# Second-layer logits as wide matmuls in one PSUM bank, W2's preparation later, and more attention weights made ahead

## The chip, the cores and the metric

One core of a Trainium2 chip. The metric is device time in microseconds (us) of one execution of the whole program; three runs of the kernel before gave 1488.98, 1492.28 and 1493.37, median 1492.28.

## The reference, cut to what matters

A graph attention network of two layers and then a mixture-of-experts feed-forward block, both added to their input. N = 1250 nodes, 20,000 edges and a self loop for each node, D = 768 features.

```python
def _gat_layer(x, src, dst, W, a_src, a_dst, bias, concat):
    N = x.shape[0]
    H, C = a_src.shape                    # layer 1: 4 heads of 512; layer 2: 1 head of 768
    h = (x @ W).reshape(N, H, C)
    al_s = jnp.einsum('nhc,hc->nh', h, a_src)
    al_d = jnp.einsum('nhc,hc->nh', h, a_dst)
    e = jax.nn.leaky_relu(al_s[src] + al_d[dst], NEG_SLOPE)
    m = jax.ops.segment_max(e, dst, num_segments=N)
    ex = jnp.exp(e - m[dst])
    denom = jax.ops.segment_sum(ex, dst, num_segments=N)
    alpha = ex / (denom[dst] + 1e-16)
    out = jax.ops.segment_sum(h[src] * alpha[:, :, None], dst, num_segments=N)
    ...
h   = jax.nn.elu(_gat_layer(x, src, dst, W1, att_src1, att_dst1, b1, concat=True))
out = _gat_layer(h, src, dst, W2, att_src2, att_dst2, b2, concat=False)
```

The change concerns the hand-over between the layers: the second layer's logits `al_s` and `al_d`, and the preparation of W2. As `h @ W2` is only needed for its product with the two attention vectors, the kernel computes `v = W2 @ a` once and gets the logits as `h1 @ v`, from the first layer's output `h1`, without the projection.

## The kernel before, in words

All edges are held in a dense count matrix CT (node by node), so attention is a dense matmul: P is the exponential of the leaky sum, times CT, and a head's output is P times its projected features. Every large f32 operand is split into a high and a low f16 half, and a product is three matmuls (`mm3`: high by high, high by low, low by high).

Nodes are ten tiles of T = 125. The destinations of a head are three blocks of 500, 375 and 375 columns (`DB`, and `TB` in tiles: four, three and three). A head's period has NG = 15 groups on TensorE: for each block one group of denominators (20 matmuls against ones) and four of attention (CH = 4 chunks of 128 features, each 30 matmuls). Groups 0, 5 and 10 are the denominators. Before the groups of head h, TensorE projects head h + 1 (`proj`); the last head has none ahead of it. Each group writes one of four banks in turn, so TensorE may be four groups ahead of VectorE, which reads them (`den_read`, `att_read`).

The order of work on each engine is written out by hand; an engine does its list in order, and waits on semaphores.

- `p_steps(h, n)` makes n more steps of P for head h: one step is a tile of 125 sources by one block, 30 tiles in 32 steps of a pipeline that goes ScalarE (L913, sum), VectorE (L1306, leaky maximum), ScalarE (L919, exponential), VectorE (L1314, times the counts), ScalarE (L931, high half), VectorE (L1321, low half). `CUR_STEPS[h][g]` says how many steps of the present head are made in group g, `NEXT_STEPS[g]` how many of the next.
- For an attention group VectorE divides (L1357), ScalarE makes a relu and an exponential (L956, L958), VectorE the ELU (L1364), ScalarE and VectorE the high and low half of h1 (L969, L1372) into `H1O`, of which there are two, one for each block in turn. SP stores them to memory (L569), and ScalarE waits for the store of two blocks ago and for `al2` of it before it writes again.
- `chain_row`, `chain_max` (L1285, ten a head) and `chain_shift` (L1291 to L1295) make the next head's row of logits and the shift of the softmax, over TensorE's transposes (L1690, L1694) and SP's broadcasts through memory. TensorE's transpose for the shift stands in front of group 8. P of the next head can begin when the shift rows are back.
- `al2(k)` is the second layer's logits of block k (12 in all): for each tile of the block and each of the four chunks, three matmuls of the 128 by 125 part of h1 against the two columns of `V2S`, into bank 4. VectorE adds them to `A2C` (`a2_add`, L1380). It stands in front of the third group (c == 1) of the next block.
- `load_w2(ch)` (SP, L597), `w2_hi(ch)` (ScalarE, L977) and `w2_lo(ch)` (VectorE, L1385) bring one of W2's 16 chunks of 128 rows into one of three slots `W2G` and split it. `w2_at` places them: seven in groups 8 to 14 of the last but one head, nine in groups 0 to 8 of the last. A slot is loaded again once the chunk three before it is split.
- Behind attention TensorE projects h1 by W2, tile by tile (96 matmuls of 384 columns for each of ten), the first tile chunk by chunk as the split ones come. `al2` of the last block stands in the middle of the first tile (chunk 8), the transpose for the second layer's row (`chain_row(H)`) at its chunk 12, that for the shift behind the third tile. Then VectorE's `chain_max(H, j)` needs the masks, which SP loads into the place of the W2G slots, so behind the last `w2_lo`. SP's list also loads h1 back, tile by tile (L658).

After that come the second attention, the router and the nine feed-forward networks, which the change does not touch.

## Time and profile before

| | |
|---|---|
| median of three runs | 1492.28 us |
| profiled execution, its own time | 1488.8 us |
| its span | 1487.0 us |
| mean granted TensorE clock | 0.94 |
| TensorE matmuls busy | 1290.4 us, 87% |
| VectorE busy | 931.1 us, 63% |
| ScalarE busy | 595.8 us, 40% |
| narrow logit matmuls, 480 | 37.6 us busy |

"Busy" is the union of an engine's instructions. A row of the timeline merges instructions of one line that follow each other; its first number is where it starts in the span, its second how long it lasts, and the brackets say how long the engine stood idle before it and who released it. The granted clock is a share of 2.4 GHz: 0.5 is the lower of its two levels, 1.2 GHz, and a value between is a mean over time.

### The profile page before, as it was taken

Reading aid. Unit: us, or ns where it says so; the run is one execution under the profiler, and the core shown is the slowest. Engines: PE = TensorE matmul, PEld = TensorE weight load, DVE = VectorE, ACT = ScalarE, POOL = GpSimd, SP = SyncE. Lnnn points to the kernel's source line nnn. Section 1 sums busy time; section 2 is a strip of 40 time slices with the busy share of each in tenths; the row PEclk is TensorE's granted clock in tenths of the full one; section 3 lists DMA queues with packets and bytes.
Section 4 is the critical chain, followed back from the end, with each engine's and each line's share of the span. In section 5 each row is a group of like instructions: output and inputs, shape, how many; then the busy total and the mean of one; then the engine's idle time right before and its main releaser. Section 6 shows DMA issues by size and latency. Waiting matters only on the chain.

```text
span 1487.0 us, 19887 instructions
## 1 busy us (share of the span) xinstructions
PE 1290.4 (87%) x7482; PEld 843.1 (57%) x7482; DVE 931.1 (63%) x1863; ACT 595.8 (40%) x1025; POOL 256.5 (17%) x187
## 2 busy tenths in 40 slices
PE   1574897678899898986889999999999989999996
PEld 1342344335555565553357888888854756666664
DVE  6578996599788968867872446335468623333330
ACT  1344215566565455537752046300141124444441
POOL 1398200000000000000000000040001453344322
PEclk9987899798899899998889999999989989999999
DMA  8442201413520353134123431061220267667622
GB/s 206 166 147 78 69 0 46 135 45 110 153 92 29 103 152 94 36 87 125 54 98 103 151 117 56 16 194 35 81 86 1 61 204 190 175 181 179 165 57 29
DMA packets 71441, 152.71 MB, mean 103 GB/s; under 512 B 10837, under 2 KB 34901, under 8 KB 70730
## 3 DMA queue, kind: packets, MB, share of 16 engines
q1 hardware_dynamic: 64699, 134.28, 30.2%
q0 software_dynamic: 6656, 17.26, 6.0%
q8 instruction: 57, 0.93, 0.3%
q14 instruction: 29, 0.24, 0.1%
HBM read 118.93 MB, written 34.59 MB: 103 GB/s over the span
## 4 chain that ended last, share of the span: by engine, by line
PE 55%; DVE 17%; ACT 8%; issue 7%; DMA 6%; POOL 5%; SPq 1%; DVEq 0%; POOLq 0%; ACTq 0%
PE PS L1650 41%; PE PS L1767 5%; PE PS L1713 5%; DVE sb L1285 3%; POOL sb L762 3%; DVE sb L1306 2%; DVE sb L1314 2%; DVE sb L1194 1%; DMA sb<-in_x_dram 1%; ACT sb L931 1%; DVE sb L1321 1%; DMA h_d<-sb 1%; ACT sb L919 1%; ACT sb L913 1%; DVE sb L1357 1%
## 5 line engine op out<-in xcount | busy, mean ns | idle before, releaser
L1650 PE MATMUL PS<-sb,sb 128*125 128x384 f16 (+9 forms) x4884 | 822.4, 326 | 84.7 <-DVE sb L1199 25.9
L1650 PEld LDWEIGHTS PS<-sb,sb 128*125 128x125 f16 (+3 forms) x4884 | 579.1, 132 | 318.5 <-issue 71.7
L1767 PE MATMUL PS<-sb,sb 125*128 125x375 f16 (+1 forms) x1440 | 277.7, 356 | 0.0
L1767 PEld LDWEIGHTS PS<-sb,sb 125*128 125x128 f16 x1440 | 146.2, 102 | 124.8 <-issue 20.9
L774 POOL TENSOR_TENSOR sb<-sb,sb 125x768 f32<-125x768 f32 x10 | 18.0, 1840 | 807.7 <-DMA sb<-in_x_dram 807.7
L919 ACT ACTIVATE sb<-sb 125x375 f32<-125x375 f32 (+1 forms) x150 | 81.6, 544 | 112.8 <-DVE sb L1306 112.3
L1494 DVE SCALAR_TENSOR_TENSOR sb<-sb,sb 128x2304 f16<-128x2304 f32 x27 | 68.8, 2557 | 89.2 <-ACT sb L1052 89.2
L1713 PE MATMUL PS<-sb,sb 125*125 125x500 f16 x320 | 88.6, 417 | 12.6 <-DVE sb L1237 12.6
L1306 DVE SCALAR_TENSOR_TENSOR sb<-sb,sb,sb 125x375 f32<-125x375 f32 (+1 forms) x150 | 95.8, 640 | 3.3 <-ACT sb L913 2.9
L1237 DVE TENSOR_SCALAR sb<-sb,sb 125x500 f16<-125x500 f16 x320 | 95.5, 383 | 3.3 <-PE PS L1713 3.3
L913 ACT ACTIVATE sb<-sb,sb 125x375 f32<-125x375 f32 (+1 forms) x150 | 93.7, 628 | 8.0 <-DMA sb<-aa_d 8.0
L1194 DVE CUSTOM_DVE_ANT_0 sb<-PS,sb 125x512 f16<-125x512 f32 x80 | 55.2, 690 | 55.7 <-ACT sb L871 54.3
L1314 DVE SCALAR_TENSOR_TENSOR sb<-sb,sb 125x375 f32<-125x375 f32 (+1 forms) x150 | 87.7, 584 | 1.2 <-ACT sb L919 1.1
L1321 DVE TENSOR_TENSOR sb<-sb,sb 125x375 f16<-125x375 f32 (+1 forms) x150 | 87.9, 586 | 0.3
L762 POOL TENSOR_TENSOR sb<-sb,sb 128x768 f32<-128x768 f32 x32 | 78.0, 2470 | 55.7 <-DMA sb<-in_L_gnn_W_dram 47.6
L931 ACT ACTIVATE sb<-sb 125x375 f16<-125x375 f32 (+1 forms) x150 | 81.8, 545 | 12.0 <-DVE sb L1314 11.7
L1285 DVE CUSTOM_DVE_ANT_0 sb<-sb,sb 125x1250 bf16<-125x1250 bf16 x50 | 71.1, 1456 | 17.3 <-ACT sb L988 10.1
L1713 PEld LDWEIGHTS PS<-sb,sb 125*125 x320 | 40.1, 141 | 60.9 <-issue 40.9
L794 POOL TENSOR_TENSOR sb<-sb,sb 128x392 f16<-128x392 f32 (+2 forms) x33 | 30.8, 932 | 203.4 <-ACT sb L1070 203.4
L1624 DVE TENSOR_TENSOR sb<-PS,sb 128x588 f16<-128x588 f32 x32 | 23.8, 767 | 66.3 <-ACT sb L1092 66.3
L956 ACT ACTIVATE sb<-sb,sb 128x375 f32<-128x375 f32 (+1 forms) x48 | 30.8, 642 | 80.8 <-DVE sb L1357 80.7
L1070 ACT ACTIVATE sb<-sb 128x392 f16<-128x392 f32 (+2 forms) x33 | 17.7, 536 | 108.6 <-DVE sb L1515 108.6
(185 smaller groups left out, 1092.9 us busy)
## 6 DMA issues: line engine op xcount, KB each, us to landing
sb<-in_L_ffn_w_dram SPq DMA_DIRECT2D x24, 1152.0 KB, 5.7
sb<-xt_d SPq DMA_DIRECT2D x40, 375.0 KB, 3.9
sb<-in_L_gnn_W_dram SPq DMA_DIRECT2D x32, 384.0 KB, 3.2
sb<-mask_d SPq DMA_DIRECT2D x20, 546.9 KB
sb<-h_d SPq DMA_DIRECT2D x10, 1000.0 KB, 5.4
h_d<-sb SPq DMA_DIRECT2D x16, 375.0 KB, 5.0
sb<-aa_d SPq DMA_DIRECT2D x5, 1093.8 KB
sb<-in_L_gnn_W_dram SPq DMA_DIRECT2D x18, 256.0 KB, 3.8
```

The costliest lines, as they stand in the source:

```text
L762: nc.gpsimd.tensor_tensor(VP[a][:, :], WV[ch % 3][:, :], A2R[:, a, :], ALU.mult).then_inc(s_vp, 1)
L913: A(TMP[:, q % NTMP, 0:n], ROW[:, 1, lo:lo + n], ACT.Identity, bias=ALF[:, h, i:i + 1]).then_inc(s_p1, 1)
L919: A(TMP[:, q % NTMP, 0:n], TMP[:, q % NTMP, 0:n], ACT.Exp).then_inc(s_p3, 1)
L931: A(P[:, i, 0, lo:lo + n], TMP[:, q % NTMP, 0:n], ACT.Copy).then_inc(s_p5, 1)
L1237: V.tensor_scalar(OR[:, n % RO, :], iok[:, :], 1000.0 * c, KEY[:, bass.ds(col, 1)], ALU.add, ALU.is_equal).then_inc(s_or, 1)
L1285: V.tensor_tensor_reduce(junk, mask, max_row(h), 1.0, 3.0 * NEG, ALU.add, ALU.max, MX[:, j:j + 1]).then_inc(s_mu, 1)
L1306: V.scalar_tensor_tensor(TMP[:, q % NTMP, 0:n], ROW[:, 0, lo:lo + n], AL[:, 0, h, i:i + 1], TMP[:, q % NTMP, 0:n], ALU.add, ALU.max).then_ ...
L1314: V.scalar_tensor_tensor(TMP[:, q % NTMP, 0:n], TMP[:, q % NTMP, 0:n], 1.0, CT[:, i, lo:lo + n], ALU.min, ALU.mult).then_inc(s_p4, 1)
L1321: V.tensor_tensor(P[:, i, 1, lo:lo + n], TMP[:, q % NTMP, 0:n], P[:, i, 0, lo:lo + n], ALU.subtract).then_inc(s_p6, 1)
L1650: ins = M(out_, lhs(a), rhs(b), start=first and a + b == 0, stop=last and a == 1)
L1713: ins = M(PS[0:T, c, 0:KC], OL[:, bass.ds(col, 1), :], OR[:, n % RO, :], start=q == 0, stop=q == len(jobs[c]) - 1)
L1767: ins = M(PS[:, t, 0:n], hb[:, i, pa, 128 * c:128 * c + 128], P[:, i, pb, lo:lo + n], start=i == 0 and pa + pb == 0, stop=i == NT - 1 and ...
```

## The change

1. `al2(k)` turns its operands round: `V2S`, set into a row of 20 columns of which only 8 to 11 are not zero, is the stationary operand with 12 columns, cut so that block b's four sums (high and low part of two vectors) land on partitions 4b to 4b + 3; the moving operand is h1, with all tiles of the block (500 or 375 columns) at once. A block is 8 matmuls, and all 12 blocks are added up in bank 4, with no read between. `a2_add` and `A2C` are gone. It now stands in front of the block's fifth group (c == 3).
2. At the end, VectorE copies the 12 by 500 sums (`A2W`), ten f32 matmuls with a selection matrix `SEL` (made by GpSimd at the start) turn them into columns, and VectorE scales these. These matmuls stand in the second tile of the second projection (chunk 2), `chain_row(H)` at its chunk 6; `al2` of the last block at chunk 4 of the first tile.
3. W2's chunks 0 to 7 are split in groups 7 to 14 of the last head, 8 to 15 behind the last group. SP's loads, stores and the loads of h1 are put in another order to match.
4. The last head's P: 13 steps made in the period before instead of 9, then 2 instead of 4 before its groups, then 3, 3, 3, 3, 2, 2, 2 instead of 4, 4, 3, 3, 3, 3.

```diff
-    V2S = small([128, NCH, 2, 2], F16)
+    V2S = small([128, NCH, 20], F16)
+    SEL = small([12, NB, 2], F32)
...
-                     [4, 4, 3, 3, 3, 3, 0, 0, 0, 0, 0, 0, 0, 0, 0]]
+                     [3, 3, 3, 3, 2, 2, 2, 0, 0, 0, 0, 0, 0, 0, 0]]
...
-        NEXT_STEPS = [0, 0, 0, 0, 0, 0, 0, 0, 0, 0, 1, 2, 2, 2, 2]
+        NEXT_STEPS = [[0, 0, 0, 0, 0, 0, 0, 0, 0, 0, 1, 2, 2, 2, 2],
+                      [0, 0, 0, 0, 0, 0, 0, 0, 0, 0, 1, 2, 2, 2, 2],
+                      [0, 0, 0, 0, 0, 0, 0, 0, 0, 0, 2, 2, 3, 3, 3]]
+        W2_EARLY = 8
...
-            if h == H - 2:
-                return range(g - 8, g - 7) if g >= 8 else range(0)
-            if h == H - 1:
-                return range(min(7 + g, NCH), min(8 + g, NCH))
+            if h == H - 1 and g >= NG - W2_EARLY:
+                return range(g - NG + W2_EARLY, g - NG + W2_EARLY + 1)
+            if h == H:
+                return range(W2_EARLY, NCH)
...
             load_ht(0)
+            for ch in range(6, 8):
+                load_w2(ch)
             store_h1(NB * H - 2)
+            for ch in range(8, 11):
+                load_w2(ch)
             load_ht(1)
+            load_w2(11)
+            store_h1(NB * H - 1)
+            for ch in range(12, NCH):
+                load_w2(ch)
+            load_ht(2)
             sp.wait_ge(s_w2l, NCH)
             for t in range(2):
                 load_masks(H, t)
-            store_h1(NB * H - 1)
             chain_row(H)
-            load_ht(2)
             load_ht(3)
...
-                    p_steps(h, 4)
+                    p_steps(h, 2)
...
-                    if c == 1 and NB * h + b:
-                        a2_add(NB * h + b - 1)
...
+            for ch in w2_at(H, 0):
+                w2_lo(ch)
+            dve.wait_ge(s_a2, NB * H)
+            V.tensor_copy(A2W[:, :], PS[0:12, 4, 0:500]).then_inc(s_a2r, 1)
+            dve.wait_ge(s_a2c, 1)
+            AC = PS[0:T, 5, 0:2 * NT].rearrange("p (j a) -> p a j", a=2)
+            V.tensor_scalar(AL[:, :, H, :], AC, 1.0 / (SX * SW), None, ALU.mult).then_inc(s_a2r, 1)
             chain_row(H)
...
                 pe.wait_ge(s_y6, CH * (k + 1))
-                if k:
-                    pe.wait_ge(s_a2r, k)
-                for j in range(len(TB[b])):
-                    for c in range(CH):
-                        ins = mm3(PS[0:T, 4, 2 * j:2 * j + 2], lambda a: H1O[k % 2][:, a, j, c, :],
-                                  lambda r: V2S[:, CH * h + c, r, :], c == 0, c == CH - 1)
+                for c in range(CH):
+                    for part in range(2):
+                        ins = M(PS[0:12, 4, 0:n], V2S[:, CH * h + c, 8 - 4 * b:20 - 4 * b],
+                                H1O[k % 2][:, part, 0:nj, c, :], start=k + c + part == 0,
+                                stop=k == NB * H - 1 and c == CH - 1 and part == 1)
                 ins.then_inc(s_a2, 1)
+
+            def al2_columns():
+                pe.wait_ge(s_a2r, 1)
+                for b in range(NB):
+                    for j in TB[b]:
+                        lo = T * (j - TB[b].start)
+                        ins = M(PS[0:T, 5, 2 * j:2 * j + 2], A2W[:, lo:lo + T], SEL[:, b, :], start=True, stop=True)
+                ins.then_inc(s_a2c, 1)
...
-                    if c == 1 and NB * h + b:
+                    if c == CH - 1 and NB * h + b:
                         al2(NB * h + b - 1)
...
-                        if ch == NCH // 2:
+                        if ch == 4:
                             al2(NB * H - 1)
-                        if ch == NCH - 4:
+                    if j == 1:
+                        if ch == 2:
+                            al2_columns()
+                        if ch == 6:
                             chain_row(H)
```

Elsewhere, SP's list for the last two heads loses the loads of chunks 3 to 15 (chunks 3 to 5 stand behind the store of the last head's first block), and a constant of the expert stage (`io392`) moves to a place that is free by then.

## Rows read from the trace of the kernel before

**Rows 1.** The page's chain that ended last, shares of the span by engine.

```profile
PE 55%; DVE 17%; ACT 8%; issue 7%; DMA 6%; POOL 5%; SPq 1%; DVEq 0%; POOLq 0%; ACTq 0%
```

**Rows 2.** Busy time by stretch, us: PE, PEld, DVE, ACT, POOL, PEclk, DMA share, GB/s.

```profile
654.00:694.00 40.00, 36.79 (x233) 22.45 (x232) 21.50 (x36) 19.98 (x35) 0.00 (x0) 0.91 0.52 147
694.00:715.00 21.00, 8.00 (x25) 1.86 (x23) 19.03 (x33) 16.75 (x32) 0.00 (x0) 0.65 0.32 93
```

**Rows 3.** Timeline of TensorE, heads 1 and 2: start, us, what, count, idle before.

```profile
470.88 2.19 PE L1650 MATMUL PS<-sb,sb 128*125 128x2 f16 x36
...
502.74 5.28 PE L1650 MATMUL PS<-sb,sb 128*125 128x2 f16 x48 [2.70 <-DVE sb L1372]
507.88 7.14 PE L1767 MATMUL PS<-sb,sb 125*128 125x375 f16 x30
...
518.11 11.40 PE L1767 MATMUL PS<-sb,sb 125*128 125x375 f16 x60
...
564.46 4.07 PE L1650 MATMUL PS<-sb,sb 128*125 128x512 f16 x18 [2.72 <-DVE sb L1199]
...
653.62 9.72 PE L1767 MATMUL PS<-sb,sb 125*128 125x375 f16 x60
...
674.55 2.61 PE L1650 MATMUL PS<-sb,sb 128*125 128x2 f16 x36 [3.21 <-DVE sb L1372]
```

**Rows 4.** The same view for the last head and the first projection tile.

```profile
704.24 1.01 PE L1762 MATMUL PS<-sb,sb 125*128 125x500 f16 x2 [4.09 <-DVE sb L1321]
...
714.83 7.66 PE L1767 MATMUL PS<-sb,sb 125*128 125x500 f16 x30
...
724.39 19.14 PE L1767 MATMUL PS<-sb,sb 125*128 125x500 f16 x90
...
758.33 5.28 PE L1650 MATMUL PS<-sb,sb 128*125 128x2 f16 x48 [6.83 <-DVE sb L1372]
763.47 16.91 PE L1767 MATMUL PS<-sb,sb 125*128 125x375 f16 x90
...
790.27 14.56 PE L1767 MATMUL PS<-sb,sb 125*128 125x375 f16 x90
804.66 13.95 PE L1650 MATMUL PS<-sb,sb 128*125 128x384 f16 x108
```

**Rows 5.** Timeline of VectorE: the divisions that begin a group, heads 1 and 3.

```profile
479.46 0.68 DVE L1357 TENSOR_TENSOR sb<-PS,sb 128x500 f32<-128x500 f32 x1 [2.84 <-PE PS L1767]
...
551.16 0.55 DVE L1357 TENSOR_TENSOR sb<-PS,sb 128x375 f32<-128x375 f32 x1
...
556.19 0.55 DVE L1357 TENSOR_TENSOR sb<-PS,sb 128x375 f32<-128x375 f32 x1
...
743.68 0.67 DVE L1357 TENSOR_TENSOR sb<-PS,sb 128x500 f32<-128x500 f32 x1
...
751.78 0.67 DVE L1357 TENSOR_TENSOR sb<-PS,sb 128x500 f32<-128x500 f32 x1
```

**Rows 6.** Timeline of ScalarE: the first W2 chunk, in head 2.

```profile
669.35 0.84 ACT L977 ACTIVATE sb<-sb 128x768 f16<-128x768 f32 x1 [7.93 <-DMA sb<-in_L_gnn_W_dram]
```

**Rows 7.** Groups by line: busy us, mean ns; idle before and its releasers.

```profile
L762 POOL TENSOR_TENSOR sb<-sb,sb 128x768 f32<-128x768 f32 x32 | 78.0, 2470 | 55.7 <-DMA sb<-in_L_gnn_W_dram 47.6 <-ACT sb L875 8.1
...
L1385 DVE SCALAR_TENSOR_TENSOR sb<-sb,sb 128x768 f16<-128x768 f32 x16 | 15.3, 959 | 18.0 <-ACT sb L977 18.0
...
L977 ACT ACTIVATE sb<-sb 128x768 f16<-128x768 f32 x16 | 13.2, 827 | 7.9 <-DMA sb<-in_L_gnn_W_dram 7.9
...
L1718 PE MATMUL PS<-sb,sb 125*128 125x1 f32 x2 | 0.4, 260 | 1.1 <-DVE sb L1245 1.1
```

**Rows 8.** The 16 loads of W2 chunks (line 597), from issue to landing.

```profile
DMA to landing us min/median/max: 2.8/3.4/8.2
```

**Rows 9.** Timeline of VectorE: a mask wait, and what follows the layer-two shift.

```profile
834.89 1.46 DVE L1285 CUSTOM_DVE_ANT_0 sb<-sb,sb 125x1250 bf16<-125x1250 bf16 x1 [4.37 <-DMA sb<-mask_d]
...
846.60 0.95 DVE L1443 SCALAR_TENSOR_TENSOR sb<-PS,sb 125x768 f16<-125x768 f32 x1
```

More of the change, by code:

```diff
@@ L132, in build @@
     assert o <= 207008, o
+    A2W = at(o_a - 2016, [12, 500], F32)
     WV = [at(o_e + 3072 * b, [128, D], F32) for b in range(3)]
@@ L185, in build @@
     ones = small([T, 128], F16)
-    io392 = small([T, SLOTS], F16)
+    io392 = at(o_w2s + 30720, [T, SLOTS], F16)
     io8 = small([T, E], F32)
@@ L197, in build @@
     V2F = small([128, NCH, 2], F32)
-    V2S = small([128, NCH, 2, 2], F16)
+    V2S = small([128, NCH, 20], F16)
+    SEL = small([12, NB, 2], F32)
     AL = small([T, 2, H + 1, NT], F32)
     ALF = small([T, H + 1, NT], F32)
-    A2C = small([T, 2 * NT], F32)
     MX = small([T, NT], F32)
@@ L346, in build @@
         s_a2 = sem("al2_part_done")
-        s_a2r = sem("al2_part_added")
+        s_a2r = sem("al2_rows_kept_then_scaled")
+        s_a2c = sem("al2_columns_done")
+        s_vs = sem("v2_split")
         s_w2g = [sem(f"w2_in_slot{b}") for b in range(3)]
@@ L628, in _ @@
                             load_xt(h + 2, i)
-                    else:
-                        for ch in range(3, 7):
-                            load_w2(ch)
                     store_h1(NB * h + 1)
                 else:
-                    for ch in range(7, 10):
-                        load_w2(ch)
                     store_h1(NB * h - 1)
-                    for ch in range(10, 14):
-                        load_w2(ch)
                     store_h1(NB * h)
-                    for ch in range(14, NCH):
+                    for ch in range(3, 6):
                         load_w2(ch)
@@ L752, in _ @@
                                 allow_small_or_imprecise_dtypes=True))
+            link(nc.gpsimd.memset(SEL[:, :, :], 0.0))
+            for part in range(2):
+                link(nc.gpsimd.affine_select(out=SEL[:, :, :], in_=SEL[:, :, :], compare_op=ALU.not_equal, fill=1.0,
+                                             base=-2 * part, pattern=[[-4, NB], [-1, 2]], channel_multiplier=1))
             pool.wait_ge(s_a2v, 32)
@@ L1021, in h2_hi @@
                   scale=1.0 / SW).then_inc(s_h2h, 1)
+            for ch in w2_at(H, 0):
+                w2_hi(ch)
             act.wait_ge(s_wrl, 16)
@@ L1268, in _ @@
             dve.wait_ge(s_va, 2 * NCH)
-            link(V.tensor_copy(V2S[:, :, 0, :], V2F[:, :, :]))
-            link(V.tensor_tensor(V2S[:, :, 1, :], V2F[:, :, :], V2S[:, :, 0, :], ALU.subtract))
-            link(V.memset(A2C[:, :], 0.0))
+            link(V.memset(V2S[:, :, :], 0.0))
+            link(V.tensor_copy(V2S[:, :, 8:10], V2F[:, :, :]))
+            V.tensor_tensor(V2S[:, :, 10:12], V2F[:, :, :], V2S[:, :, 8:10], ALU.subtract).then_inc(s_vs, 1)
             def chain_max(h, j):
@@ L1373, in h1_lo @@
                                        SX, H1O[k % 2][:, 0, 0:nj, c, :], ALU.mult, ALU.subtract).then_inc(s_y6, 1)
-            def a2_add(k):
-                j0, nj = TB[k % NB].start, len(TB[k % NB])
-                dve.wait_ge(s_a2, k + 1)
-                if k:
-                    dve.wait_ge(s_a2r, k)
-                V.tensor_tensor(A2C[:, 2 * j0:2 * j0 + 2 * nj], A2C[:, 2 * j0:2 * j0 + 2 * nj], PS[0:T, 4, 0:2 * nj], ALU.add
-                                ).then_inc(s_a2r, 1)
             def w2_lo(ch):
@@ L1393, in _ @@
                 else:
-                    p_steps(h, 4)
+                    p_steps(h, 2)
                 maxed = 0
@@ L1428, in _ @@
                         w2_lo(ch)
-            a2_add(NB * H - 1)
-            dve.wait_ge(s_a2r, NB * H)
-            link(V.tensor_scalar(AL[:, 0, H, :], A2C[:, 0:2 * NT:2], 1.0 / (SX * SW), None, ALU.mult))
-            V.tensor_scalar(AL[:, 1, H, :], A2C[:, 1:2 * NT:2], 1.0 / (SX * SW), None, ALU.mult).then_inc(s_a2r, 1)
-            dve.wait_ge(s_a2r, NB * H + 1)
+            for ch in w2_at(H, 0):
+                w2_lo(ch)
[4 more added lines that the diff above has]
+            V.tensor_scalar(AL[:, :, H, :], AC, 1.0 / (SX * SW), None, ALU.mult).then_inc(s_a2r, 1)
             chain_row(H)
@@ L1775, in al2 @@
                 h, b = divmod(k, NB)
+                n, nj = DB[b][1], len(TB[b])
                 pe.wait_ge(s_y6, CH * (k + 1))
-                if k:
-                    pe.wait_ge(s_a2r, k)
-                for j in range(len(TB[b])):
-                    for c in range(CH):
-                        ins = mm3(PS[0:T, 4, 2 * j:2 * j + 2], lambda a: H1O[k % 2][:, a, j, c, :],
-                                  lambda r: V2S[:, CH * h + c, r, :], c == 0, c == CH - 1)
-                ins.then_inc(s_a2, 1)
+                if k == 0:
+                    pe.wait_ge(s_vs, 1)
+                for c in range(CH):
+                    for part in range(2):
+                        ins = M(PS[0:12, 4, 0:n], V2S[:, CH * h + c, 8 - 4 * b:20 - 4 * b],
+                                H1O[k % 2][:, part, 0:nj, c, :], start=k + c + part == 0,
+                                stop=k == NB * H - 1 and c == CH - 1 and part == 1)
+                ins.then_inc(s_a2, 1)
+            def al2_columns():
[5 more added lines that the diff above has]
+                ins.then_inc(s_a2c, 1)
             for h in range(H):
```

12 lines of the change are left out of this document (6 added, 6 removed).

## The prediction

> **What bounds the kernel now.** I read the page's chain first: TensorE holds 55% of it, VectorE 17%, ScalarE 8% and unexplained "issue" 7% [rows 1]. So TensorE sets the end, and the only gains are stretches where it stands idle or is slow. The table by stretches shows the largest near the change [rows 2]: in the first 21 us of the last head TensorE is busy 8.0 us while VectorE is busy 19.0 and ScalarE 16.8, where the 40 us before it were nearly full. TensorE's timeline then gives each wait [rows 3, 4], VectorE's what held it [rows 5]. The reader should see three kinds. (a) Heads 0 to 2: the narrow logit matmuls wait for VectorE's last H1 piece (2.70 and 3.21 us), and group 8 waits for the softmax shift. (b) The last head's denominators wait for P (rows such as 704.24, idle 4.09), because P's makers were late: at 669.35 ScalarE had stood 7.93 us for the first W2 chunk from memory [rows 6], and each later group carries a W2 pair of 0.83 and 0.96 us [rows 7]. (c) A 6.83 us idle before the logit matmuls at 758.33. From 758 to the end of attention, 804.7, nothing but clock is lost. I write head 3 for the last head, group 0 to 14 for a head's attention groups; groups 0, 5 and 10 are denominators.
>
> **Price of the logit matmuls.** Narrow ones: 36 take 2.05 us (470.88 to the next start at 472.94, 57 ns each), 48 take 2.7; 6.8 us a head. The wide ones are in no row. Nearest are attention's own with the same 500 or 375 columns: 90 in 19.14 us, 0.21 each, and 90 in 14.56, 0.16 each [rows 4]. I take those: 8 make 1.7 us, 8 short ones 1.3, so 4.3 a head. Below, they could not well beat the narrow ones' 57 ns each (0.5 us a block); above, the f32 row of 260 ns each at one column [rows 7] would be 2.1 us a block. On the path that is under 1 us a block either way. VectorE's twelve little adds (0.15 us each by its timeline, 1.8 in all) go for nothing, since most lie beside waits. The three new GpSimd instructions and the wider split vectors stand early, ahead of work that waits 47.6 us for memory [rows 7]: nothing.
>
> **Heads 1 and 2 up to the shift.** VectorE is the bound there: after 479.46 it runs nearly without a break to the shift that releases TensorE at 518.1. But at 479.46 it stood 2.84 us for TensorE's group 2, in front of which lay the narrow block of 2.05 us [rows 3, 5]. The block moves to group 4, where VectorE is behind TensorE, so VectorE gains min(2.05, 2.84) = 2.05 us in each of heads 1 and 2, 4.1 in all. The wait of 2.70 before the block at 502.74 goes too, but gains nothing: what is late next is the shift. TensorE will stand idle there about 12 us where it had 2.7 and 3.0.
>
> **Behind the shift** the tail is TensorE's. Before it held one narrow block (2.05), now two wide ones (1.7 + 1.3): +0.95 a head. The clock is the larger matter. After 2.70 us idle the rows at 502.74 and 507.88 are 2.6 and 2.3 us longer than at full speed; after 6.83 us idle the rows at 758.33 and 763.47 are 2.6 and 2.35 longer. I take 4.5 us of such loss behind each new idle (bounds 0.1, the row 653.62 against 9.6, and 7, above any row). Behind the shift it was 1.8 in head 1 (518.11: 11.40 against 9.6) and 0.1 in head 2. Head 1: +0.95 + 2.7 = +3.65, against a projection wait of 2.72 (564.46) and a little more behind it [rows 3], which were VectorE's and come earlier with the shift: about nothing left. Head 0 has no block in group 2 and no such gain; I charge it 0.5 (bounds 0 and 5). So at the shift of head 2 the kernel is 4.1 - 0.5 = 3.6 us early: 649.9.
>
> **Head 2's tail.** The first W2 pairs leave it. TensorE: six groups of 4.8, denominators 3.2, two blocks 3.0, clock 4.4: it is through at 649.9 + 39.4 = 689.3, before the 694 of then. VectorE makes P: reads group 8 at 659.7, group 9 at 666.2, denominators at 669.6, group 11 at about 675. A group with two P steps of 500 columns and no weight work takes 5.03 us (551.16 to 556.19 [rows 5]); 1.4 of it is the group's own three operations, so a third step adds 1.8: 6.9. Group 12 at 680, 13 at 687, 14 at 693.8. The tenth tile of P, which the denominators need, is done in group 14, at 698.7; they end about 699.7, where before they ended at 715.0. TensorE still waits some 6 us here, with 13 steps made ahead instead of 9.
>
> **Head 3.** From 699.7 TensorE has 7.66 (first group, as at 714.83, clock included), 19.1, 22.4 and 22.4 for the rest, and blocks 1.3 + 1.7 + 1.3: 75.9, end at 775.6. Is anything later than that? VectorE starts group 0 at 704 with 3.2 + 3 steps; groups with three steps of 375 columns and a W2 pair last 8.1 us (743.68 to 751.78), the pair is about 1.6 of it (0.83 and then 0.96, a little overlapped), so 6.5 without. It reaches group 5 at 736, where TensorE is at 731 and may be four groups ahead; with 15 steps done at 704 and three or two a group, the P tiles for group 5 are done by 720, those for group 10 by 747 (needed at 751). W2 pairs ride in groups 7 to 14, of which each leaves 4.8 us for 4.5 of VectorE's and ScalarE's turn. So TensorE holds. The idle of 6.83 and its 4.95 us of slow clock are gone. Attention ends 804.8 - 775.6 = 29.2 us earlier.
>
> **Behind attention.** The last block is wide: -0.75. Ten small f32 matmuls for the columns: 0.26 us each at most [rows 7], half when packed: +2.0 (bounds 1 and 3). Then the W2 chunks 8 to 15. They pass through three slots, each reload waits for the pair three chunks back; SP also puts a 1 MB load of H1 and a store of 0.75 MB between chunks 10 and 12. Landing takes 2.8, 3.4 or 8.2 us (least, median, most [rows 8]). TensorE uses a chunk each 0.98 us (804.66: 108 instructions less the narrow 2.05 is 11.8 for 12 chunks) and would end the first tile 17.0 after attention. Pair 7 is done at +4.8, pairs 8 and 9 at +5.8 and +6.7, 10 at +10.3. With 3.4 for every load, chunk 15 comes at +18.2, a stall of 2.2; with 8.2 for every one, at +29, a stall of 13. I take 5.5 (the loads beside the 1 MB land late, the others near the median), and 2 for clock behind short waits. In the Trainium skill, "DMA: Bandwidth & Descriptors", section "Anatomy of one DMA", a transfer costs a fixed 2.0 us and bytes over 436 GB/s, an estimate of 2.9 us for a chunk of 0.39 MB. The least landing of the trace, 2.8, agrees; by it alone this stall would be 1.3 instead of 5.5.
>
> Last, the shift of layer two. Its row now leaves from chunk 6 of the second tile instead of chunk 12 of the first: 10 chunks less, 9.8 us, to the end of the third tile, where TensorE wants the shift. Before, VectorE was done at 846.6 [rows 9] and TensorE came at 853.8, 36 chunks of 0.98 behind 818.6 [rows 4]: 7.1 us to spare. That is 2.7 short, but the mask waits in it, 4.37 us and a shorter one, lay behind two H1 loads of 1 MB, of which one is now earlier; I take 0.5 (bounds 0 and 5). Sum behind attention: -0.75 + 2.0 + 5.5 + 2 + 0.5 = +9.25.
>
> **Sum.** 29.2 - 9.25 = 20.0 us less. The profiled execution (1488.8, span 1487.0) becomes 1468.8. It lay 3.5 us, 0.2%, under the median of the runs, 1492.28, so the median becomes 1472.
>
> **Rivals.**
> - The ring of three W2 slots: landings near 8.2 us through the stall, 13 + 5 for clock, and the shift 3 late. For it: chunk 0 took that long [rows 6, 8]. Against: most took 3.4. 29.2 - 22 = 7: 1485.
> - Better: landings near 2.8, full clock, shift in time: behind attention +3: 1466, or 1463 if the clock comes back sooner behind the shifts.
> - Slower: P still binds the last head. Its 33 steps are as many as before; four more are squeezed into head 2's tail, and if groups with three steps need 8 to 9 us there, the tenth tile comes no earlier than it did, and VectorE's lag carries through groups 5 and 10. Then 3.6 is gained in front and 9.25 lost behind: +5.6, 1498. It decides from the point at which head 3 gives back less than 9.25 - 3.6 = 5.7 us. Against: the 8.1 us groups had a W2 pair, and VectorE's three operations a step add to 1.8.
> - Slower also: the clock. The idle before each shift grows from 2 to 4 us to 9 to 12. If the clock stayed at 1.2 GHz for the whole 35 us tail of the three heads, 17.5 each instead of 4.5, less some 5 of slack: 1506. The rows show no low stretch over 10.5 us behind an idle. In the Trainium skill, "TensorE: Matmul & The Clock Gate", section "Part 1: The HAM clock gate", the half clock is the default state, which activity releases; read so, the length of the idle does not matter, the loss is as in the rows, and the sum stands.
>
> **Chances.** Forecast 0.58 (its own range 1466 to 1479); slot ring 0.17; better 0.12; P still binding 0.08; clock 0.05. The range takes in the ring and the better case: 1463 to 1485. A measurement of this kernel tells about 0.3%, 4.5 us, from nothing. Faster: the first three but for 0.02 of the ring's far end, plus mild forms of the last two, 0.86; same 0.05; slower 0.09.
>
> **What would show it.** Right: group 2's read on VectorE with under 1 us idle in heads 1 and 2; an idle of 9 to 12 us before each shift; no W2 line in head 2; the last head's denominators ending near 700; attention ending near 776; waits for the W2 pair (VectorE) in the first projection tile of 3 to 8 us; TensorE's wait at the layer-two shift under 3. Wrong: idle before group 5 or 10 of the last head; over 10 us lost in the first projection tile; a clock under 0.8 over a whole tail.

## The result, and the profile after

Four runs of the changed kernel gave a median of 1469.28 us (1465.73 to 1471.1), four of the kernel before on the same chip 1491.58: ratio 0.9848, 95% interval 0.9824 to 0.9872. The forecast was 1472. The profiled execution took 1465.73 us, its span is 1463.9, 23.1 less than before. The page's chain by engine has TensorE at 60% where it had 55 [rows 1]; its matmuls are busy 1267.5 us, 87% of the span.

The stretches of [rows 2], after:

```profile
654.00:694.00 40.00, 36.78 (x219) 20.50 (x216) 30.75 (x53) 27.87 (x53) 0.00 (x0) 1.00 0.41 107
694.00:715.00 21.00, 20.90 (x92) 9.27 (x92) 20.80 (x38) 16.66 (x36) 0.00 (x0) 0.92 0.11 37
```

In the second, TensorE is busy 20.90 of 21 us instead of 8.00. VectorE and ScalarE do about as much there as before: they are no longer late, since their busy time in the first stretch rose from 21.5 and 20.0 us to 30.8 and 27.9.

TensorE's timeline of head 1 (lines: L1771 attention, L1766 denominators, L1786 the wide block, L1698 the shift's transpose, L1654 projections), for [rows 3]:

```profile
483.79 1.45 PE L1786 MATMUL PS<-sb,sb 128*12 128x375 f16 x8
...
516.05 0.38 PE L1698 MATMUL PS<-sb,sb 125*20 125x125 f32 x1 [11.63 <-DVE sb L1308]
516.22 6.95 PE L1771 MATMUL PS<-sb,sb 125*128 125x375 f16 x30
523.10 1.86 PE L1786 MATMUL PS<-sb,sb 128*12 128x500 f16 x8
```

Head 2's tail and the last head, for [rows 4]:

```profile
649.08 0.38 PE L1698 MATMUL PS<-sb,sb 125*20 125x125 f32 x1 [8.80 <-DVE sb L1308]
649.25 6.99 PE L1771 MATMUL PS<-sb,sb 125*128 125x375 f16 x30
...
686.65 3.54 PE L1766 MATMUL PS<-sb,sb 125*128 125x500 f16 x16
692.07 0.59 PE L1766 MATMUL PS<-sb,sb 125*128 125x500 f16 x2 [1.89 <-DVE sb L1335]
694.10 0.79 PE L1766 MATMUL PS<-sb,sb 125*128 125x500 f16 x2 [1.43 <-DVE sb L1335]
694.68 20.68 PE L1771 MATMUL PS<-sb,sb 125*128 125x500 f16 x90
...
740.62 1.87 PE L1786 MATMUL PS<-sb,sb 128*12 128x500 f16 x8
742.42 4.95 PE L1771 MATMUL PS<-sb,sb 125*128 125x375 f16 x30
```

From 694.68 no row of the last head has a wait (the first 90 matmuls lose 1.5 us of clock). The waits have moved to two other places: one long idle before each shift, and the first projection tile, which before had none in 13.95 us [rows 4]:

```profile
771.10 4.07 PE L1654 MATMUL PS<-sb,sb 128*125 128x384 f16 x24
775.09 1.45 PE L1786 MATMUL PS<-sb,sb 128*12 128x375 f16 x8
776.47 7.04 PE L1654 MATMUL PS<-sb,sb 128*125 128x384 f16 x42
785.75 1.45 PE L1654 MATMUL PS<-sb,sb 128*125 128x384 f16 x6 [2.23 <-DVE sb L1391]
789.05 8.17 PE L1654 MATMUL PS<-sb,sb 128*125 128x384 f16 x36 [1.85 <-DVE sb L1391]
797.15 2.34 PE L1796 MATMUL PS<-sb,sb 12*125 12x2 f32 x20
799.41 5.80 PE L1654 MATMUL PS<-sb,sb 128*125 128x384 f16 x24
805.05 0.27 PE L1694 MATMUL PS<-sb,sb 125*10 125x125 f32 x1
805.16 25.51 PE L1654 MATMUL PS<-sb,sb 128*125 128x384 f16 x156
830.51 0.27 PE L1698 MATMUL PS<-sb,sb 125*20 125x125 f32 x1
```

Who held it is in ScalarE's timeline: the first half of a W2 pair waits for its chunk from memory, and VectorE's half (L1391) and TensorE wait behind.

```profile
778.75 0.84 ACT L989 ACTIVATE sb<-sb 128x768 f16<-128x768 f32 x1 [2.43 <-DMA sb<-in_L_gnn_W_dram]
783.86 0.84 ACT L989 ACTIVATE sb<-sb 128x768 f16<-128x768 f32 x1 [4.27 <-DMA sb<-in_L_gnn_W_dram]
787.16 0.84 ACT L989 ACTIVATE sb<-sb 128x768 f16<-128x768 f32 x1 [2.46 <-DMA sb<-in_L_gnn_W_dram]
```

The layer-two shift stands at 830.51, before at 853.66: 23.15 us, the whole gain of the span.

### The profile page after: what moved, and what is told of

The parts are those of the page before. It is cut to its first block, busy times and chain, and to the rows that moved or that the text cites. A ratio compares the mean times of both kernels' runs of the same rounds, so it can differ in the third digit from the quotient of the medians.

```text
span 1463.9 us, 19131 instructions
## 1 busy us (share of the span) xinstructions
PE 1267.5 (87%) x7118; PEld 814.8 (56%) x7118; DVE 931.5 (64%) x1851; ACT 595.6 (41%) x1025; POOL 257.6 (18%) x190
## 4 chain that ended last, share of the span: by engine, by line
PE 60%; DVE 17%; DMA 6%; ACT 6%; issue 5%; POOL 5%; SPq 1%; DVEq 0%; POOLq 0%; ACTq 0%
PE PS L1654 40%; PE PS L1771 10%; PE PS L1717 5%; DVE sb L1299 3%; POOL sb L774 3%; DVE sb L1320 2%; DVE sb L1328 2%; PE PS L1766 2%; DVE sb L1208 1%; DVE sb L1335 1%; DMA sb<-in_x_dram 1%; DVE sb L1251 1%; POOL sb L806 1%; DMA sb<-in_L_ffn_w_dram 1%; DVE sb L1371 1%
## 5 line engine op out<-in xcount | busy, mean ns | idle before, releaser
L1654 PE MATMUL PS<-sb,sb 128*125 128x384 f16 (+8 forms) x4404 | 790.1, 340 | 68.0 <-DVE sb L1213 23.4
L1654 PEld LDWEIGHTS PS<-sb,sb 128*125 128x125 f16 (+3 forms) x4404 | 543.7, 129 | 302.0 <-issue 70.7
L1771 PE MATMUL PS<-sb,sb 125*128 125x375 f16 (+1 forms) x1440 | 267.4, 347 | 0.0
L1771 PEld LDWEIGHTS PS<-sb,sb 125*128 125x128 f16 x1440 | 141.9, 99 | 121.9 <-issue 14.0
L1717 PE MATMUL PS<-sb,sb 125*125 125x500 f16 x320 | 88.6, 417 | 12.6 <-DVE sb L1251 12.6
L1084 ACT ACTIVATE sb<-sb 128x392 f16<-128x392 f32 (+2 forms) x33 | 17.7, 536 | 108.6 <-DVE sb L1519 108.6
L968 ACT ACTIVATE sb<-sb,sb 128x375 f32<-128x375 f32 (+1 forms) x48 | 30.8, 641 | 69.7 <-DVE sb L1371 69.7
```

The source lines that it names most:

```text
L1654: ins = M(out_, lhs(a), rhs(b), start=first and a + b == 0, stop=last and a == 1)
L1717: ins = M(PS[0:T, c, 0:KC], OL[:, bass.ds(col, 1), :], OR[:, n % RO, :], start=q == 0, stop=q == len(jobs[c]) - 1)
L1771: ins = M(PS[:, t, 0:n], hb[:, i, pa, 128 * c:128 * c + 128], P[:, i, pb, lo:lo + n], start=i == 0 and pa + pb == 0, stop=i == NT - 1 and ...
```

## The experiments

Eleven kernels ran. Each time is a median of four runs, its ratio taken against the kernel before on the same chip, whose medians were 1491.03 in the first eight and 1491.57 in the last three; brackets are 95% intervals of the ratio. The profiles differ by some us before anything that was edited (the same transpose near the start of attention comes at 270.95 in one and at 275.71 in another), so I also give distances between two marks. A head's shift is TensorE's transpose that it waits for in the middle of that head (380.07 in head 0 before, 653.51 in head 2); the layer-two shift is the one at 853.66 before.

### The two halves of the change

Wide form and later place alone; W2 and P as before.

```diff
-            if h == H - 1 and g >= NG - W2_EARLY:
-                return range(g - NG + W2_EARLY, g - NG + W2_EARLY + 1)
-            if h == H:
-                return range(W2_EARLY, NCH)
+            if h == H - 2:
+                return range(g - 8, g - 7) if g >= 8 else range(0)
+            if h == H - 1:
+                return range(min(7 + g, NCH), min(8 + g, NCH))
...
-                     [3, 3, 3, 3, 2, 2, 2, 0, 0, 0, 0, 0, 0, 0, 0]]
+                     [4, 4, 3, 3, 3, 3, 0, 0, 0, 0, 0, 0, 0, 0, 0]]
```

> The wide logit blocks in front of the fifth group, with W2's preparation and the steps of P as before (the last block, the ten column matmuls and the row's transpose at chunks 8 and 12 of the first tile and 0 of the second). My theory: the logits earn 5 us up to head 2's shift, by freeing VectorE of its wait at the third group, and part of the 11.8 us of idle and slow clock in the middle of the last head; but the first denominators of the last head still wait for P. About 1481 us (1477 to 1485), denominators of the last head ending 4 to 7 us earlier than the 715.0 of before. Rival (the gain is the matmuls' own: 480 narrow ones against 96 wide ones): nearly all of the 22 us is here, 1472 or less.

Measured 1480.25, 0.9928 [0.9913, 0.9943]: 10.8 us, inside my range, but one part of the theory fell: the last head's denominators do not end 4 to 7 us earlier. They wait as before (4.09, 3.67 and 3.22 us the longest, end about 715.7). ScalarE now stands 8.23 us for the first W2 chunk, which it halves at 670.01 (before: 7.93 us, 669.35), so what the earlier shift gave is lost there. The first projection tile has no wait. The mirror image: W2 and P as in the change, logits narrow and in front of the third group.

```diff
 # against the change; al2 and a2_add are those of the kernel before (36 or 48 narrow matmuls)
-                    if c == CH - 1 and NB * h + b:
+                    if c == 1 and NB * h + b:
                         al2(NB * h + b - 1)
```

> The other half: W2 halved in and behind the last head, P's steps as in the change, but the narrow logit matmuls in front of the third group with VectorE's adds, as before. My theory: up to head 2's shift nothing is gained (shift at 653 to 655), the last head's denominators end near 700, attention ends near 780, behind attention some 10 us are lost: about 1478 us (1474 to 1483). Rival (the matmuls' own): 1486 or more.

Measured 1468.7, 0.9851 [0.9836, 0.9867]: 22.3 us, as much as the whole change, and 9 faster than I expected. The halves bring 10.8 and 22.3, together 22.3. The distances between marks say where (us gained against the kernel before; each is one pair of profiles, and the first column varies by 2 to 3 us between kernels with the same instructions there):

| | head 0's shift to head 2's | to the last head's attention | to its end | to the layer-two shift |
|---|---|---|---|---|
| wide form and place alone | 3.0 | -2.5 | 13.9 | -1.9 |
| W2 and P alone | 2.2 | 17.7 | 10.2 | -6.5 |
| the change | 5.4 | 15.7 | 13.4 | -10.4 |

In the first two columns and the last the halves add up within about 2 us. In the third they do not: 13.9 and 10.2 make 13.4, and the 10.7 us that are missing there are about the 10.8 that are missing in the medians. It is the idle in the middle of the last head and the slow clock behind it. The narrow block there, which stood 6.83 us idle and then took 5.28 [rows 4], has in the second half no wait and takes 2.89. VectorE has no W2 pairs in front of it any more, and also fewer steps of P; which of the two frees it was not separated. The block's own price stays: with no idle before it, the 90 matmuls behind it take 16.17 us for 14.56.

```profile
732.50 2.89 PE L1657 MATMUL PS<-sb,sb 128*125 128x2 f16 x48
735.25 16.17 PE L1774 MATMUL PS<-sb,sb 125*128 125x375 f16 x90
...
775.71 12.97 PE L1657 MATMUL PS<-sb,sb 128*125 128x384 f16 x102
790.05 1.19 PE L1657 MATMUL PS<-sb,sb 128*125 128x384 f16 x6 [1.36 <-DVE sb L1390]
793.37 4.82 PE L1657 MATMUL PS<-sb,sb 128*125 128x384 f16 x18 [2.13 <-DVE sb L1390]
798.42 7.04 PE L1657 MATMUL PS<-sb,sb 128*125 128x384 f16 x42 [0.23 <-DVE sb L1390]
805.30 0.27 PE L1697 MATMUL PS<-sb,sb 125*10 125x125 f32 x1
```

So each half alone removes that idle, and together they can remove it only once. Attention ends at 775.7, 4.6 us later than in the change, and yet the row's transpose comes at 805.30 against 805.05: of the 33.9 us that the change takes from the end of attention to it, this one needs 29.6. The 4.3 are the columns (2.3) and the slow 24 matmuls behind them (5.80 against 4.1), with waits for W2 of 3.7 instead of 4.1. Which of the two matters is asked again below.

### Form and place of the logit matmuls

The place alone, in the kernel before: narrow blocks in front of the fifth group (`c == 1` becomes `c == CH - 1`, on TensorE and VectorE).

> The kernel before with only the place changed: narrow blocks and VectorE's adds in front of the fifth group. My theory: most of what the wide form earned comes from its place, so this is within 3 us of the run with the wide blocks alone: shift of head 2 at 649 to 650, about 1483 us (1480 to 1487). Two narrow blocks (4.7 us against 3.0) now stand in each tail behind the shift. Rival (the form counts): no better than 1489.

Measured 1483.57, 0.9952 [0.9938, 0.9967]: 7.5 us, two thirds of the 10.8. The form brings the other 3.3. The place takes the last head's wait away (736.59 and 762.49 have none): 10.6 us from the beginning of its attention to its end. Up to head 2's shift it brings 1.1, less than the kernels vary by, and that shift stands at 653.89, not at the 649 to 650 that I expected. The denominators wait as before. Now the form in the old place, in the change:

```diff
-                    if c == CH - 1 and NB * h + b:
+                    if c == 1 and NB * h + b:        # wide block, third group
```

> The changed kernel with the wide block back in front of the third group: only the move undone. My theory: in heads 1 and 2 the block of 1.3 us stands again in front of the group that VectorE waits for, so the shift comes 1.3 later in each, and the wait of 2 to 3 us before the block in group 7 returns, hidden before the shift: 2 to 4 us slower than the change, 1472 (1470 to 1475). Rival (the place is what counts, since the block's wait for VectorE lowers the clock of what follows): 6 or more slower, 1476. Look also at the clock: if the matmul's form counts, the attention group behind a wide block that had waited runs at full clock sooner than the 4.7 us that it ran low behind the narrow one.

Measured 1471.77, 0.9873 [0.9851, 0.9896], 2.5 us slower than the change, as expected; but its profile is 7.7 us longer behind the layer-two shift, where nothing was edited, and 3.1 us longer up to head 2's shift, inside the variation of that stretch, so the 2.5 us are not shown to be the place's. The rows of head 1, against 502.74 and 507.88 of [rows 3], are the finding:

```profile
500.28 1.87 PE L1786 MATMUL PS<-sb,sb 128*12 128x500 f16 x8 [2.64 <-DVE sb L1386]
502.08 4.95 PE L1771 MATMUL PS<-sb,sb 125*128 125x375 f16 x30
```

and the same place in the kernel with W2 and P changed and narrow blocks:

```profile
502.43 4.21 PE L1657 MATMUL PS<-sb,sb 128*125 128x2 f16 x48 [2.71 <-DVE sb L1377]
506.51 6.91 PE L1774 MATMUL PS<-sb,sb 125*128 125x375 f16 x30
```

This idle costs nothing before the wide block (granted clock 1.00 over both rows), and 1.3 + 2.0 us before the narrow one (0.66, then 0.71; at full clock the rows are 2.89 and 4.95). Head 2 agrees: behind 1.89 us of idle the wide block and the 30 take 1.86 and 4.95, behind 1.96 the narrow ones take 4.44 and 6.67. The 4.9 us of slow clock that I read in [rows 3] and priced into every new idle were not the idle's alone; they came with 48 two-column matmuls behind it. The block lowers the clock even with no idle before it: in the last head of the narrow kernel it runs at 1.00 (732.50) and the 5 us behind it at 0.66. But the wide block is not free behind every idle. In head 0 of the same run the idle is longer:

```profile
363.34 3.50 PE L1786 MATMUL PS<-sb,sb 128*12 128x500 f16 x8 [4.53 <-DVE sb L1386]
366.77 6.13 PE L1771 MATMUL PS<-sb,sb 125*128 125x375 f16 x30
```

That is 2.8 us lost; the narrow blocks there, behind the same 4.53, lose 4.0 to 4.2 (5.28, then 6.50 to 6.71). So the form saves clock at each of these places, all of it behind 1.89 and 2.64 us of idle and a part of it behind 4.53.

### P made ahead

```diff
-                     [3, 3, 3, 3, 2, 2, 2, 0, 0, 0, 0, 0, 0, 0, 0]]
+                     [4, 4, 3, 3, 3, 3, 0, 0, 0, 0, 0, 0, 0, 0, 0]]
-                       [0, 0, 0, 0, 0, 0, 0, 0, 0, 0, 2, 2, 3, 3, 3]]
+                       [0, 0, 0, 0, 0, 0, 0, 0, 0, 0, 1, 2, 2, 2, 2]]
-                    p_steps(h, 2)
+                    p_steps(h, 4)
```

> The changed kernel with P's steps as before (9 made ahead, then 4, then 4, 4, 3, 3, 3, 3); wide logits and W2 as changed. My theory: it was the W2 pairs and the wait for their first load that made P late, not the number of steps: with groups of 5.03 us and four steps behind them, the tenth tile of P is done 1 to 2 us later than in the change. About 1471 us (1469 to 1474). Rival (the steps made ahead are what closed the wait, as the prediction's working has it): the denominators of the last head end 5 to 8 us later, 1475 to 1478.

Measured 1471.52, 0.9862 [0.9835, 0.9889]; attention of the last head begins at 699.69 instead of 694.68, waits of 0.36, 1.70, 1.69, 1.10 and 0.56 before it. So the time is the one I expected, while the denominators end 5.0 us later (3.5 counted from head 2's shift), more than my 1 to 2 and at the near end of the rival's 5 to 8. In medians the steps are worth 2.2 us, between head 0's shift and layer two's 6.3 (455.7 against 449.4), which one pair of profiles can't settle. Either way most of the 20 us by which the denominators end earlier (715.0 to 694.9) come from the W2 pairs' leaving head 2: with P as before they still end near 699.9, where with the wide form alone they ended near 715.7.

### The weight pairs behind attention

Two ways to shorten the 4.1 us of waits. Twelve pairs before attention ends instead of eight:

```diff
-        W2_EARLY = 8            # one pair in each of groups 7 to 14
+        W2_EARLY = 12
+        W2_IN = [0, 0, 0, 0, 0, 0, 0, 1, 2, 1, 2, 1, 2, 1, 2]
```

> The changed kernel with twelve W2 chunks split in groups 7 to 14 of the last head (1, 2, 1, 2, ...) and four behind it. My theory: the waits for the pairs (4.1 us) and the slow clock behind them (about 4.6 us by the trace of the change) leave the first projection tile; VectorE has room in those groups. 1462 us (1459 to 1466). Rival (VectorE and ScalarE then come late with the last head's h1, TensorE waits four groups ahead and at the last logit block, and the row's chain of layer two binds anyway): no better than 1468.

Measured 1459.89, 0.9789 [0.9768, 0.9811]: 9.4 us faster than the change, of which the trace shows 6.8 between the end of attention and the layer-two shift (52.6 for 59.4). Attention ends 1.9 later, but 1.8 of it stands already at head 2's shift, before the edit. The tile has no wait, and full clock up to the columns:

```profile
778.36 13.87 PE L1654 MATMUL PS<-sb,sb 128*125 128x384 f16 x84
792.15 2.34 PE L1796 MATMUL PS<-sb,sb 12*125 12x2 f32 x20
794.42 5.79 PE L1654 MATMUL PS<-sb,sb 128*125 128x384 f16 x24
```

And the order of transfers only: H1's second load of 1 MB behind chunk 12 instead of in front of chunk 11.

```diff
+            for ch in range(11, 13):
+                load_w2(ch)
             load_ht(1)
-            load_w2(11)
             store_h1(NB * H - 1)
-            for ch in range(12, NCH):
+            for ch in range(13, NCH):
```

> The changed kernel with the second 1 MB load of h1 issued behind W2 chunk 12 instead of in front of chunk 11. My theory: chunks 11 and 12 landed late (7 and 9 us) because of it; now they land in 3.5 to 5, the first tile's waits fall from 4.1 to 1.5 or less with part of the clock: 3 us less, 1466 (1464 to 1469). Rival (the ring of three slots binds by itself, each turn being a landing and a pair): the waits stay within 1 us of 4.1.

Measured 1468.37, 0.9848 [0.9810, 0.9885]: nothing. One wait of 5.50 us takes the place of two of 2.23 and 1.85; from the end of attention to the columns it is 26.2 us against 26.05. That is neither my 1.5 nor the rival's 3.1 to 5.1. The landings say why. In the change the three chunks issued behind the 1 MB load, around the store of h1, landed in 7.1, 8.9 and 7.5 us. Here the three issued before them landed in 2.9 to 4.4, about as I had expected, and the three behind them in 8.4, 7.1 and 7.1. So it is the chunks behind these transfers that land late, and the edit only passed the delay on from chunks 11 to 13 to chunks 13 to 15. Loading h1 behind all of W2 was not tried. With twelve pairs early, ScalarE still waits 3.44 us for a chunk, but TensorE no longer waits for it.

### The idle before the shift

VectorE's copy of the logit row goes one group earlier, TensorE's transpose one later, so that a group of 30 attention matmuls fills part of the idle.

```diff
 # TensorE
+                    if h + 1 < H and g == SHIFT_AT + 1:
+                        chain_shift(h + 1)
                     if c == CH - 1 and NB * h + b:
                         al2(NB * h + b - 1)
-                    if h + 1 < H and g == SHIFT_AT:
-                        chain_shift(h + 1)
 # VectorE
-                    if h + 1 < H and g == SHIFT_AT:
+                    if h + 1 < H and g == SHIFT_AT - 1:
                         chain_shift_rows(h + 1)
```

> The changed kernel with TensorE's transpose for the next head's shift in front of group 9 instead of 8, and VectorE's copy of it behind its read of group 7 instead of 8. TensorE then does group 8 in the idle of 9 to 16 us before the shift. My theory: 4.8 us of attention moves into that idle in heads 0 to 2, and P of the next head starts some 5 us earlier, since its rows are stored earlier; 6 to 10 us less, 1461 (1458 to 1465). Rival (VectorE binds the projections behind heads 0 and 1 and P of the last head, wherever TensorE stands): within 2 us of 1469.

Measured 1456.64 (runs from 1447.38 to 1458.35), 0.9749 [0.9711, 0.9787]: 12.6 us faster than the change; I had expected 6 to 10, and 1456.64 lies below my range. From head 0's shift to layer two's the traces show 10.2. The idle falls from 15.70, 11.63 and 8.80 us to 10.93, 6.85 and 4.03; from head 0's shift to head 2's it is 259.7 us against 268.0. In head 2:

```profile
642.39 0.38 PE L1698 MATMUL PS<-sb,sb 125*20 125x125 f32 x1 [4.03 <-DVE sb L1308]
642.70 3.50 PE L1786 MATMUL PS<-sb,sb 128*12 128x500 f16 x8
646.13 5.92 PE L1771 MATMUL PS<-sb,sb 125*128 125x375 f16 x30
```

Here too a wide block stands behind an idle, 4.03 us with one transpose between, and is slow: 3.50 us for 1.87, at a granted clock of 0.50, and the 30 behind it 5.92 for 4.95 (0.83).

### Together

Both of these edits on the change.

> The change with both earlier edits: twelve weight pairs of W2 before the end of attention, and the shift row's transpose before group 9. Theory (the two gains lie in different stretches and add): attention ends at 761.4 + 1.9 = 763.3 us (the later shift's end, and what the twelve pairs cost it in the earlier run), 52.6 us from there to the layer-two shift as in the run with twelve pairs, so the shift at about 816 us against 830.5 in the change: 1450 us, 1447 to 1454. Rival (VectorE binds head 2, and the four extra pairs in its period take back what the later shift gave): attention ends at 768 or later, 1455 us or more.

Measured 1447.3 (1446.13 to 1448.45), 0.9699 [0.9671, 0.9727]: 44.3 us faster than before, 22 faster than the change. They add. From head 0's shift to layer two's it is 429.0 us, against 449.4 in the change and 473.6 before. The first tile:

```profile
757.82 4.07 PE L1654 MATMUL PS<-sb,sb 128*125 128x384 f16 x24
...
776.99 2.34 PE L1796 MATMUL PS<-sb,sb 12*125 12x2 f32 x20
779.25 4.11 PE L1654 MATMUL PS<-sb,sb 128*125 128x384 f16 x24
```

Attention ends 5.5 us earlier than I expected, of which 2.9 is an earlier start (head 0's shift at 379.8 against 382.7), and 1.9 is what I had charged for the twelve pairs, which in fact cost attention nothing; and the 24 matmuls behind the columns, which took 5.8 us in the change and in the runs with twelve pairs, the later shift and the later load, took 4.11. The run with twelve pairs has the same instructions around them and no wait in that tile either, and took 5.79. That slow stretch is not the columns' fixed price. The next kernel was planned before I had this trace; it moves the columns to where I thought they would be free of it.

```diff
-                    if j == 1:
-                        if ch == 2:
+                        if ch == 12:
                             al2_columns()
-                        if ch == 6:
+                    if j == 1:
+                        if ch == 0:
                             chain_row(H)
```

> As the run with both edits, with the columns in front of the first tile's chunk 12 and the row transpose in front of the second tile's chunk 0, as in the run with the wide form alone. Theory (the 24 matmuls behind the columns took 5.79 us at the lower clock where they stand now and 4.11 us in the run with the wide form alone): 1.7 us less than the run with both edits, about 1448 us. Rival (the columns now wait for VectorE, whose add of the last logits stands behind its pairs, and TensorE idles there): 1 to 4 us more than the run with both edits.

Measured 1452.51, 0.9739 [0.9709, 0.9769], 5.2 us slower. The rival's wait is there, at more than its 1 to 4 us: VectorE's copy of the last logits stands behind its W2 pairs, and

```profile
773.16 4.33 PE L1796 MATMUL PS<-sb,sb 12*125 12x2 f32 x20 [3.15 <-DVE sb L1436]
777.41 6.95 PE L1654 MATMUL PS<-sb,sb 128*125 128x384 f16 x24
```

3.15 us of wait, 2.0 and 2.8 of slow clock: 8.0, which is what the distance from the end of attention to the shift grew by (51.0 to 58.9). The span grew by 5.4 only, as its start was 1.9 us earlier and the part behind the shift 1.3 shorter, with the same instructions.

Last, the narrow form again, with twelve pairs early (`c == 1`, 36 and 48 matmuls), to see what it loses where W2 doesn't bind.

> Twelve pairs early as before, but the logits in their narrow form at the third group. Theory (what the wide form gains in attention, 4.65 us, is eaten by the columns and the lower clock behind them, 2.34 + 1.7 us): within 1 us of the wide form with twelve pairs, 1460.5 us, 1459 to 1462. Rival (the ring of W2's slots hid the difference of the two forms in the earlier pair of runs; with twelve pairs it no longer binds): 1464.5 us, 4.6 more than the wide form.

Measured 1468.27, 0.9840 [0.9804, 0.9876]: 8.4 us slower than the wide form with twelve pairs, which neither theory gives. In its trace attention ends 4.95 later, the row's transpose 1.4 later, the shift 2.6 later (1.11 of it a wait for VectorE), and the span is 8.3 longer. Of each of these distances 1.0 lies before head 0's shift. Up to the transpose the theory holds: the wide form's gain in attention goes for the columns and their slow stretch. The missing 5.7 us lie behind the shift, where the two kernels have the same instructions. One place of them, the kernel with narrow blocks and then the one with wide:

```profile
1128.23 1.30 PE L1893 MATMUL PS<-sb,sb 24*125 24x512 bf16 x3 [1.74 <-DVE sb L1592]
1129.46 5.78 PE L1657 MATMUL PS<-sb,sb 128*128 128x416 f16 x18
```

```profile
1124.03 0.74 PE L1903 MATMUL PS<-sb,sb 24*125 24x512 bf16 x3 [1.74 <-DVE sb L1589]
1124.69 3.34 PE L1654 MATMUL PS<-sb,sb 128*128 128x416 f16 x18
```

The same wait, and 3.0 us of slower matmuls in one only. Over all 13 profiles this later part, from the layer-two shift to the end, took 633.3 us (before) to 641.1 (wide block in third place). Why its clock falls in one program and not in another is open, and so it is open whether the wide form, with twelve pairs, is worth the 8.4 us of the medians or the 1.6 us that the traces show between head 0's shift and layer two's.

## Why the prediction was right, point by point

- **The wide block's price** (1.7 and 1.3 us): 1.87 and 1.45. Right, by rows of the same column count.
- **Heads 1 and 2** (shift of head 2 at 649.9): 649.08. From head 0's shift to it it was 273.4 us before and 268.0 after. The change and the runs of its form with P as before, W2 otherwise and the wide form alone have the same compute instructions there; they took 268.0 to 271.2, so the gain of 3.6 sits inside 2.2 to 5.4. But the two later kernels with narrow blocks in third place, the same instructions as before up to there, took 271.2 and 273.5, so these traces don't exclude a smaller gain. The step itself is shown: VectorE's wait for group 2 fell from 2.84 to 0.78 us in both heads.
- **The idle before the shift** (about 12, 9 to 12): 15.70, 11.63 and 8.80. Head 0's I had not worked out; what I charged head 0, 0.5 us, is not to be told from the variation of its start.
- **The clock behind each new idle** (4.5 us): this is the term that was mis-sized. The 30 matmuls behind the shift took 6.19, 6.95 and 6.99 us where 4.8 is full speed: 1.4 to 2.2 (up to 3.0, 7.77 us, in head 1 of the other kernels with the same instructions there). The wide-in-third-place run shows why: the rows I took it from held a block of narrow matmuls, which behind the same idle of 2.6 to 2.7 us cost 3.3 us where the wide one cost nothing, and behind 4.53 us 4.0 to 4.2 where the wide one cost 2.8. Head 2's tail took 37.6 us instead of 39.4. In the Trainium skill, "TensorE: Matmul & The Clock Gate", section "Part 1: The HAM clock gate", "the default state is throttled, and activity releases the throttle". The trace agrees so far as a longer idle did not cost more: behind 11.63 us of idle 2.1 us were lost, behind 8.80 2.2, and behind the 4.27 and 4.30 of head 1 in the two narrow kernels with W2 moved 1.6 and 3.0 (60 matmuls in 11.16 and 12.63 for 9.6). But 2.64 us before a wide block cost nothing and 4.03 cost 2.6, so not every idle has the price of the others.
- **P in head 2's tail**: groups with three steps 6.86 us (6.9), with two 5.04 (5.03). The reads of groups 8 and 9 came at 656.28 and 662.96 instead of 659.7 and 666.2, since the clock cost less (2.2 for 4.5) and the shift was 0.8 earlier, and that carried through: denominators done at 694.9, 4.8 us before the 699.7 of the sum.
- **The last head** (75.9 us, TensorE's alone): 76.4, from 694.9 to 771.3. VectorE never held it. So attention ended 33.6 us earlier, not 29.2.
- **Behind attention** (+9.25): from the end of attention to the shift 59.4 us against 49.0 (804.66 to 853.66), +10.4. Waits for W2 4.1 (5.5), columns 2.3 (2.0), slow clock 4.4 (2): six matmuls 1.45 for 0.98, 36 in 8.17 for 5.9, 24 in 5.80 for 4.1; the shift nothing (0.5), VectorE being done 0.4 before TensorE came. The clock is the second term mis-sized. The waits of 2.23 and 1.85 us cost 2.7 us more in clock, and 1.7 were lost behind the columns, in a place where the run with both edits lost nothing.
- **The landing of W2**: 2.8, 3.4 and 8.9 us (least, median, most). In the Trainium skill, "DMA: Bandwidth & Descriptors", section "Anatomy of one DMA", the fixed cost and the bytes would give an estimate of 2.9 us a chunk, and a stall of 1.3; the section gives its figures for transfers issued by GpSimd, and SyncE issues these, which the prediction did not say. The least landing agrees. The stall of 4.1 lies between that and the 13 of landings that are all late: the chunks right behind H1's load and store took 7.1 to 8.9 us, as the prediction had assumed, and there the measurement decides.

The sum came out 3 us too cautious: +4.4 in attention, -1.15 behind it. That it is no more is in part luck: a clock term too large in front and one too small behind partly cancel. What the sum didn't say is that its parts don't add: the later place of the logits and the move of W2 and P each remove the 6.83 us idle of the last head, and without the wide form the kernel is as fast, as long as only eight pairs come early; with twelve, the medians favour the wide form by 8.4 us, 5.7 of which lie where the kernels are the same.

## What to carry to other kernels

When a change has two halves that both make an engine less late, price each alone as well as together: here 10.8 and 22.3 us made 22.3. Price the clock from rows with the same kind of matmul behind the idle. A block of 48 two-column matmuls can cost clock with no idle before it (1.6 and 1.8 us behind it in four of six places, nothing in two). And when the idle has only moved (here to the shift, and to weights loaded through three slots), the next gain lies there: a group in front of the late transpose and four pairs more under attention brought 22 us more.

## What the runs showed that I had not expected

- Behind the same idle of 2.6 to 2.7 us, eight matmuls of 500 columns and the 30 after them ran at full speed (1.87, 4.95 us); 48 of two columns took 4.21, 4.57 or 5.28 us in three kernels where 2.89 is full, and the 30 after them 6.91, 6.53 or 7.14 where 4.95 is. Behind 4.03 and 4.53 us the wide block lost clock too (3.50, then 5.92 and 6.13).
- W2 chunks issued right behind a 1 MB load of h1, around two stores of 375 KB, all by SyncE, landed in 7.1 to 8.9 us, those before them in 2.9 to 4.4.
- The speed of the same instructions differs between programs: 24 matmuls behind the columns took 4.11 us in two traces and 5.8 in six. Of these eight, only the 5.79 with twelve pairs, the 4.11 with both edits and the 4.11 with the wide form alone have no wait in that tile. With the later part's 633.3 to 641.1 us this makes a single profile of such a kernel uncertain by several us, more than most edits of one place are worth.
